# A routed network after cross-attention: the pads of the expert lists zeroed three batches ahead, and the first tiles' rows loaded before the block ends

## The reference

```python
# cross-attention: 16 heads of 16, keys and values from ctx (32, 1444, 256)
x = x + tanh(g_xattn) * (softmax(Q(layernorm(x)) K(ctx).T / 4) V(ctx)) @ Wo.T
# routed network: 12 experts, 3 chosen per row
h = layernorm(x)
probs = softmax(h @ Wr + br); top_vals, top_idx = top_k(probs, 3); ew = softmax(top_vals)
for e in range(12):
    w_e = mean of ew over the rows that chose e
    out += mask_e * w_e * (relu(h @ w1[e] + b1[e]) @ w2[e] + b2[e])
phi = sigmoid(relu(out.mean(rows) @ Wp1 + bp1) @ Wp2 + bp2)
x = x + tanh(g_ffn) * out * (1 - 0.8 * (phi > 0.7))
```

## Time and profile before

| | |
|---|---|
| median of 3 runs | 2185.39 us (2180.34 to 9590.7) |
| the profiled execution | 2176.29 us, span 2174.6 us |
| mean granted TensorE clock | 0.983 |
| busy, share of the span | PE 96%, DVE 67%, ACT 60%, POOL 37% |
| HBM | 100.74 MB read, 41.29 MB written |

### The profile page before, as it was taken

The page is one execution under the profiler, slowest core; times in us unless marked ns, Lnnn a source line. Parts: engine busy times, 40 slices in busy tenths (PEclk is TensorE's granted clock), DMA queues, the critical chain, the costliest instruction groups (busy, mean ns, idle before and its releaser), DMA issues. The chain is left out here.

```text
span 2174.6 us, 63929 instructions
## 1 busy us (share of the span) xinstructions
PE 2084.3 (96%) x24158; PEld 1847.2 (85%) x24158; DVE 1464.7 (67%) x3319; ACT 1308.7 (60%) x3073; POOL 806.2 (37%) x1188
## 2 busy tenths in 40 slices
PE   6999999999999999999999999999999599999994
PEld 5788888888888888888888888888887499999994
DVE  6777777777777877777777777777775333333333
ACT  2465666666666665666656666665665377777771
POOL 4334433333444333443333444333331133433341
PEclk9999999999999999999999999999999799999996
DMA  6655555555555555555555555555546744333334
GB/s 169 155 136 139 138 137 142 136 139 136 135 138 142 143 139 137 136 134 138 138 143 140 145 133 139 139 136 141 139 126 233 235 122 103 57 60 61 61 52 136
DMA packets 228271, 288.53 MB, mean 133 GB/s; under 512 B 83416, under 2 KB 154428, under 8 KB 227708
## 3 DMA queue, kind: packets, MB, share of 16 engines
q1 hardware_dynamic: 202524, 254.82, 43.8%
q0 software_dynamic: 18528, 21.64, 5.6%
q10 hardware_dynamic: 6912, 7.99, 1.3%
HBM read 100.74 MB, written 41.29 MB: 65 GB/s over the span
## 5 line engine op out<-in xcount | busy, mean ns | idle before, releaser
L693 DVE TENSOR_REDUCE max_part<-max_ps 100x1 f32<-100x512 f32 x1508 | 974.8, 655 | 349.0 <-PE max_ps L1003 319.5
L560 ACT ACTIVATE probs<-score_ps 128x400 f32<-128x400 f32 x1498 | 734.7, 504 | 411.0 <-PE score_ps L986 402.1
L986 PE MATMUL score_ps<-q_stack,k_stack 97*128 97x200 f32 (+1 forms) x2996 | 598.2, 282 | 2.7 <-DVE max_part L693 1.2
L1003 PE MATMUL max_ps<-k_stack,q_stack 96*100 96x512 f32 x1508 | 585.1, 388 | 8.3 <-DVE max_part L693 6.8
L986 PEld LDWEIGHTS score_ps<-q_stack,k_stack 97*128 97x128 f32 (+1 forms) x2996 | 463.1, 183 | 68.3 <-issue 31.8
L485 POOL TENSOR_TENSOR ctx_hi<-ctx_raw,zero_col 128x256 fp32r<-128x256 f32 (+1 forms) x384 | 213.6, 588 | 621.7 <-PE v_ps L1017 589.8
L1056 PE MATMUL pv_ps<-probs,v_ones 128*17 128x100 f32 x12288 | 304.0, 250 | 5.6 <-ACT pv_out L575 2.7
L1056 PEld LDWEIGHTS pv_ps<-probs,v_ones 128*17 128x17 f32 x12288 | 256.9, 98 | 51.7 <-issue 37.4
L1003 PEld LDWEIGHTS max_ps<-k_stack,q_stack 96*100 96x100 f32 x1508 | 252.3, 167 | 16.3 <-DVE max_part L693 11.9
L490 POOL TENSOR_TENSOR ctx_lo<-ctx_raw,ctx_hi 128x256 fp32r<-128x256 f32 (+1 forms) x384 | 259.6, 708 | 7.5
L618 ACT ACTIVATE k_hl<-k_ps,bk_c 128x512 fp32r<-128x512 f32 (+1 forms) x192 | 127.5, 664 | 211.5 <-PE k_ps L1034 189.3
(11 more groups left out here) (202 smaller groups left out, 2558.6 us busy)
## 6 DMA issues: line engine op xcount, KB each, us to landing
k_stack<-k_hl SPq DMA_DIRECT2D x496, 128.0 KB, 2.6
ctx_raw<-in_ctxT SPq DMA_DIRECT2D x64, 512.0 KB, 4.4
k_stack<-k_hl SPq DMA_DIRECT2D x496, 64.0 KB, 2.2
k_stack<-k_hl SPq DMA_DIRECT2D x252, 105.0 KB, 2.4
w_all<-in_w SPq DMA_DIRECT2D x24, 640.0 KB, 8.6
ctx_raw<-in_ctxT SPq DMA_DIRECT2D x32, 420.0 KB, 4.8
k_stack<-k_hl SPq DMA_DIRECT2D x252, 52.5 KB, 2.0
x_t<-rows_by_expert SPq DMA_DIRECT2D x86, 134.5 KB, 2.2
```

The lines of the kernel that those rows point to most:

```text
L560: act.activation(probs[0:tw, n % PROBS, :], score_bank(n)[0:tw, 0:UH * SQ], ACT.Exp, scale=SCALE).then_inc(exp_done, 1)
L693: dve.tensor_reduce(max_part[b % 2][:, h, j:j + 1], max_bank(m)[0:SQ, 0:CW[j]], AX.X, ALU.max).then_inc(max_read, 1)
L986: ins = pe.matmul(score_bank(n)[0:TW[i], 2 * SQ * p:2 * SQ * (p + 1)], k_stack[b % 2][:, 2 * u + p, 128 * i:128 * i + TW[i]], q_stack[b % ...
L1003: pe.matmul(max_bank(m)[0:SQ, 0:CW[j]], q_stack[b % 3][0:96, h // 2, SQ * (h % 2):SQ * (h % 2) + SQ], k_stack[b % 2][0:96, h // 2, k0[j]:k ...
```

## The change

1. The pads' position is computed in slot 384 instead of 404 and waits for batch 28's counts instead of batch 30's. As the rows of three batches (29 to 31) may still land behind it, 428 zero rows are written for each expert (`LATER = 3 * SQ + RT`) instead of 256. They are written as 107 partitions of four rows each instead of 128 partitions of two.
2. SP writes all twelve in slot 384, behind the weights of experts 0 to 2. ACT writes none.
3. POOL waits for the twelve before it scatters batch 29 instead of batch 31.
4. The four row loads of the first four tiles move from the start of the second block to the end of the first, on SP: it waits for the table (`tiles_listed`), reads the four places, waits until every row is scattered, and sends the four loads. `x_t` gets a fixed place in SBUF, behind the expert weights, in the room of the keys of batch 31.

```diff
-REGION = B * SQ + 2 * RT
+REGION = B * SQ + RT
+LATER = 3 * SQ + RT
+AHEAD = 5
...
-PAD_SLOT = NT * (B - 1) + AT_PV + 11
+PAD_SLOT = NT * B
...
-                                     max_val=NE * REGION - 2 * RT)
-                eng.dma_start(xs[bass.ds(row, 2 * RT), :].rearrange("(r p) d -> p r d", p=128),
-                              zero_rows.unsqueeze(1).broadcast_to([128, 2, XW])).then_inc(cleared, 16)
+                                     max_val=NE * REGION - LATER)
+                eng.dma_start(xs[bass.ds(row, LATER), :].rearrange("(p r) d -> p r d", r=4),
+                              zero_rows[0:LATER // 4].unsqueeze(1).broadcast_to([LATER // 4, 4, XW])).then_inc(cleared, 16)
...
                 if g == PAD_SLOT:
-                    clear_pads(sp, range(0, 9))
+                    clear_pads(sp, range(NE))
+            sp.wait_ge(tiles_listed, 1)
+            first_rows = [sp.value_load(table[0:1, TILES + t:TILES + t + 1], min_val=0, max_val=NE * REGION - RT)
+                          for t in range(AHEAD - 1)]
+            sp.wait_ge(scattered, 16 * TOPK * B)
+            for t, row in enumerate(first_rows):
+                sp.dma_start(x_t[t][:], xs[bass.ds(row, RT), :]).then_inc(rows_in[t], 16)
             sp.wait_ge(x1_stored, 16 * B)
...
-                    if b == B - 1:
+                    if b == B - 3:
 
                         pool.wait_ge(cleared, 16 * NE)
...
-                    if b == B - 1:
-                        clear_pads(act, range(9, NE))
...
+                if g == PAD_SLOT + 1:
+                    dve.wait_ge(small_done, SMALL_NO["pads", 0] + 1)
+                    dve.tensor_tensor(table[0:1, 3 * TILES:], small_ps[0:1, 0:NE], base[0:1, :],
+                                      ALU.add).then_inc(small_read, 1)
...
-                    pe.wait_ge(counted, B)
+                    pe.wait_ge(counted, B - 2)
...
-            for t in range(AHEAD - 1):
-                load_rows(t)
```

More of the change, by code:

```diff
@@ L55 @@
 FIRST_EXPERTS = 10
+ROWS_AT = 4 * XW + 12
 AT_XQ, AT_MAX, AT_NEG, AT_SCORE, AT_PV, AT_POST = -5, 6, 18, 20, 21, 33
@@ L111, in program @@
         b2_w = nc.alloc_sbuf_tensor_at("b2_w", [128, NE + 1, D], F32, offset=first + ROOM)
+        x_t = [nc.alloc_sbuf_tensor_at(f"x_t{p}", [128, XW], F32,
+                                       offset=first + ROOM + 4 * (NE + 1) * D + ROWS_AT * p) for p in range(AHEAD)]
+        rows_in = [ctx.enter_context(nc.semaphore(f"x_in{p}")) for p in range(AHEAD)]
         attention(nc, x, ctxT, g_xattn, wqT, bq, wkT, bk, wvT, bv, woT, bo, wr, br,
-                  xs, ys, x1s, qd, table, wexp, w_all, b2_w, w1, b1, w2, b2)
-        experts(nc, xs, ys, x1s, table, wexp, w_all, b2_w, g_ffn, w1, b1, w2, wp1, bp1, wp2, bp2, out)
+                  xs, ys, x1s, qd, table, wexp, w_all, b2_w, x_t, rows_in, w1, b1, w2, b2)
+        experts(nc, xs, ys, x1s, table, wexp, w_all, b2_w, x_t, rows_in, g_ffn, w1, b1, w2, wp1, bp1, wp2, bp2, out)
 def attention(nc, x, ctxT, g_xattn, wqT, bq, wkT, bk, wvT, bv, woT, bo, wr, br,
-              xs, ys, x1s, qd, table, wexp, w_all, b2_w, w1, b1, w2, b2):
+              xs, ys, x1s, qd, table, wexp, w_all, b2_w, x_t, rows_in, w1, b1, w2, b2):
     with ExitStack() as ctx:
@@ L288, in attention @@
         table_done = sem("table_done")
+        tiles_listed = sem("tiles_listed")
         cleared = sem("cleared")
@@ L961, in _ @@
             dve.wait_ge(table_done, 1)
-            step(dve.tensor_copy(table[0:1, 0:3 * TILES].rearrange("p (i t) -> p i t", i=3),
-                                 small_ps[0:1, 0:3 * 128].rearrange("p (i t) -> p i t", i=3)[:, :, 0:TILES]))
+            dve.tensor_copy(table[0:1, 0:3 * TILES].rearrange("p (i t) -> p i t", i=3),
+                            small_ps[0:1, 0:3 * 128].rearrange("p (i t) -> p i t", i=3)[:, :, 0:TILES]).then_inc(tiles_listed, 1)
         @block.tensor
@@ L1150, in _, with experts @@
             ins.then_inc(table_done, 1)
-def experts(nc, xs, ys, x1s, table, wexp, w_all, b2_w, g_ffn, w1, b1, w2, wp1, bp1, wp2, bp2, out):
+def experts(nc, xs, ys, x1s, table, wexp, w_all, b2_w, x_t, rows_in, g_ffn, w1, b1, w2, wp1, bp1, wp2, bp2, out):
     with ExitStack() as ctx:
@@ L1163, in sem @@
             return ctx.enter_context(nc.semaphore(name))
-        AHEAD, OUT, SLOTBUFS = 5, 4, 6
+        OUT, SLOTBUFS = 4, 6
         PARTS, TPP = 5, B * SQ // 128
         STORES = [1, 2, 4, 6, 6, 6]
-        sb("room_of_weights", [128, ROOM // 4 + (NE + 1) * D])
+        sb("room_of_weights", [128, ROOM // 4 + (NE + 1) * D + AHEAD * ROWS_AT // 4])
         ident = sb("ident2", [128, 128])
@@ L1174, in experts @@
         w2_c = [sb(f"w2_c{p}", [128, FM, D]) for p in range(2)]
-        x_t = [sb(f"x_t{p}", [128, XW]) for p in range(AHEAD)]
         xT = sb("xT", [128, KD, RT])
@@ L1207, in experts @@
         own = sem("own2")
-        x_in = [sem(f"x_in{p}") for p in range(AHEAD)]
         late_in = {e: sem(f"late_in{e}") for e in range(FIRST_EXPERTS, NE)}
@@ L1303, in load_rows @@
                 sp.wait_ge(always, 1)
-                sp.dma_start(x_t[t % AHEAD][:], xs[bass.ds(row, RT), :]).then_inc(x_in[t % AHEAD], 16)
-            for t in range(AHEAD - 1):
-                load_rows(t)
+                sp.dma_start(x_t[t % AHEAD][:], xs[bass.ds(row, RT), :]).then_inc(rows_in[t % AHEAD], 16)
             for e in range(FIRST_EXPERTS, NE):
```

8 lines of the change are left out of this document (2 added, 6 removed).

## The result

Six runs of the changed kernel gave a median of 2441.64 us (2437.87 to 2444.99); six runs of the kernel before beside them gave 2183.2 (without one far outlier, 9590.7, 2179.9 to 2185.39). The ratio is 1.1194, with a 95% interval of 1.1179 to 1.1208. The forecast was 2415.9 us in a range of 2395 to 2465. The profiled execution took 2439.77 us.

A forecast was written before the change was run, and what follows sets the result against it. PE (TensorE), busy 96% of the span, was taken as the bound, so its waits add to the time. 230.6 + 1.0 + 0.3 - 1.4 = +230.5 on the median 2185.4 gave 2415.9 us, range 2395 to 2465.

The forecast's parts named there:

- the slack of 1.1 us: Batch 31's row of maxima lands at 1670.0; PE's first scores of batch 31 need it and start at 1671.13.
- How many engines serve a clear: Clears in slot 384: 107 partitions, being prime, put all 428 packets of each clear on one DMA engine.
- The order of transfers: On SP's queue transfers are served in order, so the row of maxima waits behind the clears; another queue's don't block.
- Term 1: Before batch 31's scores: PE waits for the row of maxima behind 5136 packets at 45.2 ns, +230.6 us.
- the low row: Packet price from 16 engines moving 1024 B: 43.0 ns, or 45.2 ns for 1076 B; a lone engine was put nearer this.
- The high price: Rival for the clears: one engine at 64.3 ns a packet, 330.2 us in place of 232.1, 2514 us; chance 0.04.
- Term 2: POOL waits for clears before batch 29's scatter: nothing added, covered by PE's own stall; without that cover 4 us.
- Term 3: Slot 392 after the stall: PE's clock at 0.50 makes it slower, +1.0 us, between 0 and 3.
- Term 4: The pads' matmul (0.34 us) moves into slot 384: +0.3 us if PE is full there, 0 otherwise.
- Term 5: End of attention: earlier transposes and scatter, rows already loaded, first expert matmul earlier: -1.4 us, between -3.3 and 0.

The follow-up runs named there:

- 112 in the later place: Changed kernel with 112-partition clears of 448 rows, sent by SP in slot 390 behind batch 31's row of maxima: 2197.76 us, without early row loads 2201.23 us.
- the run with ACT's row: Changed kernel with batch 31's row of maxima sent from ACT's queue instead of SP's, clears still 107 partitions in slot 384: 2429.5 us, ratio 1.1151.

## Why the prediction was right, and by how much its terms were off

*What bounds the kernel, and the slack of 1.1 us.* Right. The row of maxima became the wait that ends last, and nothing absorbed it.

*How many engines serve a clear.* Right, and shown: stalls of 259, 130 and 21 us for 107, 86 and 112 partitions, with shares of 7.0% and 14.3% for the first two and 100.4% for 112 in the later place. The step from four transfers of 76 partitions to 107 held.

*The order of transfers.* The outcome held; the picture was wrong. The forecast had the row sent early and waiting in the queue with a landing of over 200 us. In fact SP's sends themselves were held. From the third clear (1689.05) to the twelfth (1886.3) one began every 21.9 us, and a clear takes 428 x 51.06 ns = 21.9: one goes out as one is finished. That is why x_res and x1 were blocked as well, as the run with ACT's row shows. The hold is not complete: x1 and the row went out in 0.36 and 0.75 us while the last clear had some 6 us to go (the one engine's 21 GB/s lasts until about 1935.5). How much a queue takes before it holds its sender was not measured. The forecast also says that another queue's transfers don't block them; they don't, but they share: with two queues on the one engine, a clear took twice as long.

*Term 1, the stall.* This is the mis-sized term. 45.2 ns a packet, taken from sixteen engines fed with 1024 B and scaled, should have been 51.06. 5136 x 51.06 ns = 262.2 us in place of 232.1: +30.1 us. PE's idle time was 259.2 where 230.6 stood, +28.6. The whole change was forecast at +230.5 and came to +258.4 in the medians, a miss of 27.9; the absolute time is off by only 25.7 (2441.6 against 2415.9), since the kernel before came out at 2183.2 and not at 2185.4. The argument that a lone engine is nearer to the low row, since it shares nothing, pointed the right way and still lost a third of the distance between 45.2 and 64.3. The high price, 64.3, was near what sixteen engines showed: 65.6 ns with 112 partitions. The range held, because its upper end was worked out with 54.7 ns.

*Term 2, POOL's wait, at nothing.* Right in this kernel only because PE stalled at the same time. Take the stall away, and PE's next wait is for what stands behind this one on POOL's queue: 253.7 us with 107 partitions, 17.9 with 112. The forecast gave "4 us of the three scatters" as the price without cover; that was far too low, because it left out the clears themselves, which the wait is for.

*Term 3, the clock, +1.0.* It came out at -0.2. From slot 392's scores to batch 31's third group of products with the values (pv) it takes 12.70 us before (1671.13 to 1683.83) and 12.49 after (1936.19 to 1948.68). The granted clock was 0.50 in part of it before as well (1676 to 1682); after, it was 0.50 from 1935 to 1946 and 0.99 from there to 1949. The term charged half clock against a full-clock slot that the kernel before didn't have.

*Term 4, the pads' matmul, +0.3.* It came out at nothing: slot 384 begins 5.75 us later than before and ends 5.75 later (PE's first scores 1648.53 and 1654.28, its last key block's 1651.60 and 1657.35), with the matmul in between.

*Term 5, the end, -1.4.* The transposes of pv_out came 0.87 us earlier behind the last pv group (0.35 expected): ACT's copy began 1.97 us behind the start of that group instead of 2.56, and the table's add no longer stands between. The scatter starts 1.62 us behind the count instead of 3.39; the forecast took 2.95 us off, and 1.8 came off. The first expert matmul is 0.66 us nearer to the count, where -1.4 less those 0.35 were expected, about -1.05. Together with term 3 these are -1.7 from slot 392's start to the end of the span, where +1.0 and -1.4, so -0.4, stood.

So: slot 392 begins 265.06 us later, 5.74 of them drift, which leaves 259.32; less 1.66 behind it (501.81 us to the end instead of 503.47) that is 257.7 us in the profiles, 258.4 in the medians. The mechanism and the sign of the whole were right; the one large price came out 13% higher than it was put.

## What to carry to other kernels

Choose the number of partitions of a transfer by its largest divisor up to 16 before anything else: twenty more rows of zeros in each clear cut PE's wait from 259 to 21 us here. Before moving a group of sends up a queue, list what stands behind it on that queue and on every queue that waits for it; here three different waits (the row of maxima, POOL's inverse deviation, the store of x1) took turns as the clears moved. One order of SP's queue that no run tried is with x_res and x1 of the last batches ahead of the seven expert loads; whether that lets the early pads pay is open.

## What the runs showed of the hardware that was not expected

- An engine that sends transfers of 428 packets to one DMA engine was held in its sends: 20.8 us each in the median, and 41 to 43 us when SP and ACT both sent. Where sixteen engines served the clears, a send took 0.6 to 0.7 us in the median, and more than half of SP's 17 to 28 us for twelve was not spent in sends.
- One DMA engine alone moved 1076 B every 51.06 ns and 584 B every 32.95 ns (21 and 18 GB/s), two engines 1076 B every 50.9 ns each, sixteen 1041 B in the mean every 65.6 ns each (257 GB/s in all, twelve times what one moved).
- Two queues together were no faster than one on that engine: 3919 packets in 200 us against 3917.
